# Gates and five expert units of the last stage set between the last steps of the attention before it

## What is computed

```python
x = _layernorm(x + _L3_attn_ref(x, ...), axis=-1)
x = _layernorm(x + _L3_ffn_ref(x, ...), axis=-1)

# _L3_attn_ref: 16 heads of 64, relative positions clipped to 16
sim = einsum('bid,bjd->bij', q, k) * scale + einsum('btd,tsd->bts', q, k2) * scale
attn = softmax(sim)
out = einsum('bij,bjd->bid', attn, v) + einsum('bts,tsd->btd', attn, v2)
return out.reshape(...) @ Wo.T + bo

# _L3_ffn_ref: 16 routed experts of 64 hidden columns and a shared one of 128
weights, idx = _gate(x, w_gate)          # sigmoid, best 2 of 4 groups, best 4 of their experts
combine = (one_hot(idx, E) * weights[..., None]).sum(1)
g = silu(einsum('th,efh->tef', x, w1_e))
u = einsum('th,efh->tef', x, w3_e)
routed = einsum('tef,ehf,te->th', g * u, w2_e, combine)
shared = silu(x @ w1_s.T) * (x @ w3_s.T) @ w2_s.T
return routed + shared
```

## Time and profile before

| | |
|---|---|
| median of 3 runs | 2401.18 us (2400.6 to 2401.75) |
| the profiled execution | 2408.72 us, span of its records 2407.0 us |
| PE busy, share of the span | 2171.0 us, 90% |
| DVE, ACT, POOL busy | 1529.4, 1138.6, 745.6 us |
| mean granted TensorE clock | 0.954 of 2.4 GHz |

### The profile page before, as it was taken

One profiled execution on the slowest core, in us unless ns is written; L12 is line 12 of the kernel. 1 busy time (PEld: TensorE's weight loads), 2 busy tenths in 40 slices (PEclk: granted clock), 3 DMA queues, 4 the chain that ended last, 5 costly groups with the idle time before them and its releaser, 6 DMA issues.

```text
span 2407.0 us, 40343 instructions
## 1 busy us (share of the span) xinstructions
PE 2171.0 (90%) x15552; PEld 1250.4 (52%) x15552; DVE 1529.4 (64%) x3047; ACT 1138.6 (47%) x1833; POOL 745.6 (31%) x1057
## 2 busy tenths in 40 slices
PE   6986789989769888989989998998999999999888
PEld 2332456666545445545653434445666656666555
DVE  5775677777687777745557653016676767666473
ACT  2565455556415445563324545124554545545342
POOL 3644343332147664430013210003223231232033
PEclk7998899999989999999998979999999999999899
DMA  4420111111333433102012200003553544444252
GB/s 138 134 77 2 28 32 26 30 28 28 106 93 117 135 103 106 51 2 97 1 58 80 70 24 31 1 0 113 156 182 106 184 145 145 158 132 154 71 107 54
DMA packets 183975, 198.79 MB, mean 83 GB/s; under 512 B 55922, under 2 KB 152614, under 8 KB 179302
## 3 DMA queue, kind: packets, MB, share of 16 engines
q1 hardware_dynamic: 183782, 196.20, 27.2%
HBM read 93.46 MB, written 92.08 MB: 77 GB/s over the span
## 4 chain that ended last, share of the span: by engine, by line
PE 45%; DVE 5%; issue 2%; ACT 1%; DMA 1%; POOL 1%; SPq 0%; POOLq 0%; DVEq 0%; ACTq 0%
PE PS L2282 5%; PE PS L2071 5%; PE PS L2304 5%; PE PS L2289 4%; PE PS L1924 3%; PE PS L2261 2%; PE PS L1911 2%; PE PS L1914 2%; PE PS L575 2%; PE PS L2267 1%; PE PS L538 1%; PE PS L2321 1%; PE PS L557 1%; PE PS L540 1%; PE PS L2606 1%
## 5 line engine op out<-in xcount | busy, mean ns | idle before, releaser
L2427 ACT ACTIVATE AR<-PS,AR 128x512 f32<-128x512 f32 x256 | 173.5, 684 | 115.1 <-DVE AR L2365 115.0
L1253 ACT ACTIVATE AR<-PS 128x1024 f32<-128x1024 f32 x160 | 162.4, 1023 | 124.2 <-PE PS L1002 123.3
L696 ACT ACTIVATE AR<-PS 128x1024 f32<-128x1024 f32 x160 | 163.1, 1024 | 116.4 <-PE PS L561 69.6
L1106 DVE TENSOR_REDUCE AR<-PS 128x2 f32<-128x768 f32 (+1 forms) x192 | 160.0, 864 | 54.7 <-PE PS L982 27.9
L2365 DVE TENSOR_REDUCE AR<-PS 128x2 f32<-128x1024 f32 x128 | 156.8, 1225 | 11.1 <-DVE PS L2362 0.5
L2473 POOL TENSOR_TENSOR RA<-AR,RA 128x288 f32<-128x288 f32 x128 | 89.1, 696 | 236.2 <-ACT AR L2427 236.2
L2282 PE MATMUL PS<-AR 64*128 64x200 f32 (+2 forms) x1280 | 147.1, 357 | 2.2 <-ACT AR L2427 2.2
L2289 PE MATMUL PS<-CC,AR 128*128 128x128 f32 x1024 | 138.0, 278 | 1.1 <-DVE RA L2371 1.1
L2289 PEld LDWEIGHTS PS<-CC,AR 128*128 128x128 f32 x1024 | 112.6, 141 | 42.1 <-issue 37.1
L1795 POOL TENSOR_TENSOR AR<-AR 128x1024 f32<-128x1024 f32 x32 | 75.4, 2356 | 183.8 <-DVE AR L1643 183.8
L2282 PEld LDWEIGHTS PS<-AR 64*128 64x128 f32 x1280 | 103.0, 186 | 51.8 <-issue 42.9
(11 more groups left out here) (359 smaller groups left out, 5081.4 us busy)
## 6 DMA issues: line engine op xcount, KB each, us to landing
ZD<-RC SPq DMA_DIRECT2D x32, 1152.0 KB
AR<-ZD SPq DMA_DIRECT2D x32, 640.0 KB
ZP<-AR SPq DMA_DIRECT2D x128, 160.0 KB, 2.6
SP<-AR SPq DMA_DIRECT2D x40, 384.0 KB, 2.6
AR<-SP SPq DMA_DIRECT2D x128, 96.0 KB
RA<-SP SPq DMA_DIRECT2D x32, 384.0 KB
SP<-AR SPq DMA_DIRECT2D x40, 256.0 KB, 2.9
RC<-RC SPq DMA_DIRECT2D x64, 130.0 KB
```

Of the source, the lines that this page charges most:

```text
L696: e.activation(self.PT[m % 6], C.PS[:, 2 * s:2 * s + 2, :], ACT.Exp).then_inc(S["s_turned"].sem, 1)
L1106: i = e.tensor_reduce(nm[:, :, 4 * up + q:4 * up + q + 1], src[:, :, a:a + wd], AX, ALU.max, negate=True)
L1253: e.activation(self.PT[m % 6], C.PS[:, 2 * s:2 * s + 2, :], ACT.Exp).then_inc(S["s_turned"].sem, 1)
L2427: i = e.activation(self.PP[n % 5][:, hh, 16:528], C.bank[2 * (n % 2) + hh], ACT.Exp, bias=self.NMX[n % 4][:, hh:hh + 1], accum_out=self.DE ...
```

## The change

`Clipped` gives its steps behind `exp 127` (30 of them) as tail, `Routed` its first eleven as head: `gate1 0`, `hidden 0`, `gate2 0`, `hidden 1`, `gate3 0`, `hidden 2`, `gate4 0`, `gate1 1`, `hidden 3`, `gate5 0`, `hidden 4`. For them to run side by side, the tail's transposes and products take turns on banks 4 and 5 alone (bank 7 is the gates'), the first five units use banks 0 to 3 alone, and the buffers of `Routed` are laid so that what the eleven steps write lies over the attention's QT, K0, K32 and DD, which are done with after block 127. "Enter" waits for `exp 127`, the DVE step of `scores 127`, and the last user of bank 7.

```diff
--- Clipped.__init__
+        late = self.plan.index(("exp", 127)) + 1
+        self.tail = len(self.plan) - late
+        few = set(self.plan[late:])
         self.ring = Turns(self.plan, 3, {"backv": S["v_backv"], ..., "turnx": S["s_turnx"]},
+                          lambda step: range(2 if step in few else 3))
+        self.past = ((S["s_exp"], 127), (S["v_scores"], 127), self.ring.held[2])
--- Routed.__init__
+        self.SL = [cv(128, 512) for _ in range(3)]
+        assert C.used <= 3072
+        C.used = 3072
+        self.GS, self.G9 = [cv(128, 8, 512) for _ in range(2)], [cv(128, 9, 512) for _ in range(3)]
         self.CT = [cv(16, 512) for _ in range(2)]
-        self.SL = [cv(128, 512) for _ in range(3)]
-        self.GS, self.G9 = [cv(128, 8, 512) for _ in range(2)], [cv(128, 9, 512) for _ in range(3)]
         self.plan = self.order()
+        self.head = self.plan.index(("hidden", 5))
+        self.slots = Turns(self.plan, 3, {"hidden": S["v_hidden"]}, lambda step: range(2 if step[1] < 5 else 3))
--- Routed.on_tensor (on_vector and on_scalar take the bank in the same way)
-            x, th, o = C.XT[:, b, 0:512], S["t_hidden"], 2 * (n % 3)
+            x, th, o = C.XT[:, b, 0:512], S["t_hidden"], 2 * self.slots.slot[step]
-            w.wait_ge(S["s_hidden"], n - 3)
+            free = self.slots.freed(*step)
+            w.wait_ge(S["s_hidden"] if free[0] else None, *free[1:])
             e.matmul(C.bank[o], wa, x, start=True, stop=True).then_inc(th.sem, 1)
-            w.wait_ge(S["v_hidden"], n - 3)
+            w.wait_ge(*free)
             e.matmul(C.bank[o + 1], wb, x, start=True, stop=True).then_inc(th.sem, 1)
```

More of the change, by code:

```diff
@@ L2188, in __init__ @@
             S["y_band", r] = C.flag(f"y_store{r}", [(n,) for n in range(r, 128, 5)], 16)
+        late = self.plan.index(("exp", 127)) + 1
+        self.tail = len(self.plan) - late
+        few = set(self.plan[late:])
         self.ring = Turns(self.plan, 3, {"backv": S["v_backv"], "backs": S["s_backs"], "q": S["s_q"], "k": S["s_k"], "qr": S["v_qr"],
-                                         "vals": S["v_vals"], "wt": S["s_wt"], "wo": S["v_wo"], "turnx": S["s_turnx"]})
+                                         "vals": S["v_vals"], "wt": S["s_wt"], "wo": S["v_wo"], "turnx": S["s_turnx"]},
+                          lambda step: range(2 if step in few else 3))
+        self.past = ((S["s_exp"], 127), (S["v_scores"], 127), self.ring.held[2])
     def order(self):
@@ L2683, in on_vector @@
             w.wait_ge(S["t_hidden"], n)
-            e.tensor_tensor(self.G9[n // 9 % 3][:, n % 9, :], C.bank[2 * (n % 3) + 1], self.SL[n % 3], ALU.mult).then_inc(S["v_hidden"].sem, 1)
+            e.tensor_tensor(self.G9[n // 9 % 3][:, n % 9, :], C.bank[2 * self.slots.slot[step] + 1], self.SL[n % 3], ALU.mult).then_inc(S["v_hidden"].sem, 1)
         elif kind == "outward":
@@ L2711, in on_scalar @@
             w.wait_ge(S["t_hidden"], n, part=1)
-            e.activation(self.SL[n % 3], C.bank[2 * (n % 3)], ACT.Silu).then_inc(S["s_hidden"].sem, 1)
+            e.activation(self.SL[n % 3], C.bank[2 * self.slots.slot[step]], ACT.Silu).then_inc(S["s_hidden"].sem, 1)
         elif kind == "fin":
```

## The result

In the runs that timed both kernels side by side the change took 2396.16 us (median of 9, 2393.2 to 2402.97), the kernel before 2404.21 (median of 9, 2400.6 to 2411.7). The ratio is 0.9966, 95% interval 0.9952 to 0.998: 8.2 us less, between 4.8 and 11.5. Timed once more, as an unchanged copy, the change stood at 0.9976 [0.9959, 0.9993], and an unchanged copy of the kernel before at 0.999 [0.9977, 1.0004]. Forecast were 4.7 us less. So the sign was right; the size lies just outside the lower edge of the first interval and inside that of the second timing (1.7 to 9.8 us).

The account below looks back on a forecast made before the run. TensorE is busy 90%, so only idle or half-clock time can be won; `outward 0` waits for `gate6 0`'s chain. 14.1 us taken out, less 7.5 later attention and 1.9 clock, gives 4.7: 2401.2 becomes 2396.5 us, range 2394.9 to 2398.0.

Parts of the forecast that it names:

- `close 31`: Attention's tail: DMA, PE and DVE chains all end near 2275.0 us, against 2267.88 before, with no slack left.
- gap ahead of `outward 0`: PE's wait for POOL to get the experts' weights by DMA, 5.78 us, claimed to stay unchanged.
- The mechanism: Interleaving delays the attention 7.5 us but starts `gate6 0` 4.7 us earlier, and `outward 0` moves with it.
- the one stretch of 3.41 us that was counted: Behind the border's 2.8 us idle, PE runs at half clock for 3.41 us, costing 1.7 us at unit 1.
- The largest term: DVE's queue at `close 30`: six steps nobody waited for before now stand ahead, making it 8.2 us later.
- rival (b): Slips of 1 us at two or three covers, or the longest half clock, leave 1 to 3 us; chance 0.18.
- The clock behind `turnx`: Units 5 and 6 can fall into half clock ahead of `gate6 0`: 0.3 to 3.4 us lost, 1.9 taken.
- Rival (a): No clock fall behind "enter", a short one behind `turnx`: up to 7.6 us less, 2393.6; chance 0.12.
- (d): TensorE stays at half clock through the tail from its restart at the border: slower, 2406.5 us; chance 0.06.
- Rival (c): Each table load costs ACT 1.28 us beyond its row, leaving 0.8 us of gain, 2400.4 us; chance 0.05.
- The forecast time: Whole kernel: median of the runs before, 2401.2 us, less the 4.7 us gain, gives 2396.5 us.
- The end: Behind `outward 0` the rest of the kernel follows it, with no further gain counted beyond the 4.7 us.

Follow-up runs that it names:

- gates_behind: The changed kernel with `gate2 0` and `gate3 0` moved behind `sums 31`, so behind `close 30` on DVE; ratio to the kernel before 0.997 [0.9954, 0.9986].
- units_only: The changed kernel with only the five units among the attention's last steps, its gates moved behind `turnx`; ratio to the kernel before 0.9996 [0.9981, 1.0012].
- gate6_early: The changed kernel with batch 0's `gate6`, `send` and `rep` one unit earlier, behind `hidden 5`; ratio to the kernel before 0.9972 [0.9956, 0.9988].
- first order by hand: The changed kernel with interleaving begun behind `av 123`, in a hand-written order of gates, units and attention steps; ratio to the kernel before 0.997 [0.9953, 0.9988].
- border_later: The changed kernel with the interleaving begun behind `send 30` instead of `exp 127`; ratio to the kernel before 0.9973 [0.9955, 0.999].

## Why the prediction was right, and where it was off

Its steps, in us behind `exp 127`, forecast and measured (the change, then its copy):

| step | forecast | measured |
|---|---|---|
| PE idle at the border | 2.8 | 2.78, 2.77 |
| copy of `wt 30` on ACT | 2.74 | 3.29, 3.20 |
| unit 1's product on DVE | 9.89 | 9.98, 10.04 |
| `close 30` | 15.34 | 15.11, 15.16 |
| `close 31` | 24.3 | 24.28, 24.34 |
| `wo`, length | 7.2 | 7.41, 7.41 |
| `turnx` | 38.0 | 38.10, 38.15 |
| unit 5 | 39.84 | 39.46, 39.97 |
| `gate6 0` | 45.2 | 44.67, 45.07 |
| gap ahead of `outward 0` | 5.78 | 5.39, 5.65 |
| end, against before | -4.7 | -8.27, -6.19 |

*The mechanism* was right step for step. The border's gap was followed by the one stretch of 3.41 us that was counted, unit 1 came within 0.1 us, `wo` ran at full clock, and `gate6 0` is 5.0 to 5.2 us earlier where 4.7 were forecast. Most of the 0.5 us in the first profile is `turnx`: it took 0.63 us at full clock, where I had carried over its 1.08 at half clock. In the copy it ran at half clock (1.09 us), and unit 5 and `gate6 0` came within 0.15 us of the forecast.

*The largest term* had the right size, 15.3 us, and half its cause. I named the DVE queue alone. gates_behind shows PE's queue, with units 0 to 2 ahead of the product of `close 30`, as a second bound only 0.4 us below. The gates were not what cost the attention most of its 8 us there: in units_only, with no gate in the tail, `close 30` still came at 12.71 us, 5.5 us later than before. Of the 2.4 us between that and the change up to 1.7 are clock, since the border of units_only ran at full clock and that of the change had 3.41 us at half.

*`close 31`*, where three chains were to end together, came when forecast, released by PE with 0.33 us of waiting (0.34 in the copy); in gate6_early the same step waited 0.35 us for its DMA instead. So they do lie within some tenths of each other, and the slips of rival (b) did not come.

*The clock behind `turnx`*, taken in the middle between 0.3 and 3.4 us, was one short stretch in one profile and 6.8 us around `turnx` in the other. From unit 5 to `gate6 0` it was 5.21 and 5.10 us instead of 3.43 at full clock, so 1.8 and 1.7 us were lost where 1.9 were taken. But that was the middle between two cases of which neither came: the short stretch of the first profile began 1.46 us behind `turnx`, not 1.0 ahead of it, and so cost its full 1.7 us instead of 0.3. The number is in part luck. Rival (a) did not come. Nor did (d): two stretches in the tail, not a tail at half clock.

*Rival (c)*, a table load dearer than its row, is refuted by the rows of the border: the load of L2722 starts at 2249.55 and its ACTIVATE at 2250.84, 1.29 us later. The Trainium skill (ScalarE: Activation LUTs, What ACT_TABLE_LOAD costs) adds a drain of some 1380 ns to the load at every switch of the set; no such time is to be seen there. In the first order by hand the loads did cost, 1.28 us each, through what stood behind them.

*The forecast time*, 2396.5 us, lies 0.3 us from the measured median, and that is luck. It stood on three runs of the kernel before, 2401.18 us; over nine runs that kernel took 2404.21. The base was 3.0 us too low and the gain, between the medians, 3.4 us too small, and the two cancel. The largest chance, 0.50, stood on a gain that can't be told from no change, 0.43 on a clear one; it came out clear, since the interval excludes 1.

*The end* is the term that was mis-sized. The prediction had "The rest of the kernel follows `outward 0`" and gave nothing for it in the sum. It does follow, within 0.1 us as far as `outward 3`. Behind that, 1.2 us came from the last transfer, in every profile of an interleaved kernel, and 1.5 us from the clock in `outward 3`, in some. With the first of these alone the sum would be 5.1 + 1.2 = 6.3 us, as in the second pair of profiles (6.19) and near the second timing (0.9976 of 2402.23 us, 5.8). What is left of the first timing's 8.2 is within its interval; how much the layout or the share of executions with half clock late in the kernel has in it stays open. As far as the profiles show, it was a term left out of the sum, and not the mechanism, that made the gain larger than forecast.

## What to carry to other kernels

When two parts are interleaved in queues that keep their order, look at the last step of the old part that everybody waits for, and at what now stands ahead of it on each engine, not on the busiest alone: here DVE and PE were within some half a microsecond of each other, and the fillers cost 8 us at `close 30` that a start fourteen steps later gave back. What makes the filling worth while is not the work moved (five units alone won nothing) but the head of the next part's longest chain, here the gates and their DMA; put that first and the bulk where the engines really stand still. Count each function-table switch at the place where it stands in ACT's queue, with all that is queued behind it.

## What the runs showed that was not expected

- With one late packet of instructions at the very end the last transfer takes 1.2 us more (3.2 instead of 2.0 us, in the four profiles with the packet against the ten without), and it appears or vanishes with edits far away in the kernel.
- Behind the same gap of 3.18 us PE took 9.72 to 10.98 us for the same 72 products in eight profiles, with half clock among them, and 8.28 in six. At the border, a gap of 2.77 or 2.78 us came with some 3.4 us at half clock in three profiles (both of the change, gates_behind), with 6.8 in gate6_early, where it began 0.8 us ahead of PE's restart, and with none in units_only; a gap of 1.86 us in border_later was followed by 3.4 us too. So the length of the gap alone does not tell in these runs whether the clock falls. Differences of 1.5 us and less in one profile of this kernel are therefore no evidence by themselves.
- The same instructions up to `exp 127` took between 2240.9 and 2253.4 us, a spread of 12.5 us, more than the change gained.
